# Attention scores of two window pairs computed in every second step, side by side in the same PSUM banks

## What is computed

```python
xw = windows_of_16x16(group_norm(x))                # 64 windows per image
q, k, v = [layer_norm(shuffle_invert(conv3(xw, w, b))) for w, b in ...]   # 64 tokens, 128 features
attn = einsum('bhqd,bhkd->bhqk', q * SCALE, k)      # 8 heads of 16 features: the scores
attn = softmax(attn + bias)
out = einsum('bhqk,bhkd->bhqd', attn, v) @ proj_w.T + proj_b
xr = windows_back(xw + pixel_shuffle(out))
y = xr + conv3(gelu(conv3(xr, c1w, c1b)), c2w, c2b)
x = x + y
```

## Time and profile before

| | |
|---|---|
| median of 3 runs | 852.24 us (850.86 to 852.25) |
| the profiled execution, its own time | 853.24 us |
| its span on the core | 851.1 us |
| PE busy in the span | 89% |
| DVE, ACT, POOL busy | 78%, 71%, 57% |
| mean granted TensorE clock | 0.984 |
| steps 7 to 27 of image 1 (five rows of four steps) | 287.3 to 378.0 us of the span |

### The profile page before, as it was taken

How to read it: one execution, slowest core, us unless ns; L and a number is a source line. 1 busy time by engine, 2 the same in 40 slices (tenths; PEclk the granted TensorE clock), 3 DMA queues, 4 the chain that set the end, 5 groups by cost and what they waited for, 6 DMA issues and landing times.

```text
span 851.1 us, 19126 instructions
## 1 busy us (share of the span) xinstructions
PE 761.1 (89%) x5704; PEld 537.6 (63%) x5704; DVE 660.4 (78%) x2142; ACT 605.7 (71%) x1287; POOL 483.2 (57%) x1041
## 2 busy tenths in 40 slices
PE   0479999999788999999888999999989899999988
PEld 0347777766356777767445777776735677777753
DVE  6558888878657888878675888887866788888575
ACT  1498888765478888876457888877556888886651
POOL 5468677752237777764144776776233677776410
PEclk9999999999999999999999999999999999999999
DMA  7110123000231030300052013110014212000004
GB/s 250 56 29 30 48 108 106 1 1 1 87 125 55 28 128 0 106 1 2 1 166 70 29 30 126 52 55 1 1 56 137 64 34 78 0 1 2 1 1 148
DMA packets 17655, 47.14 MB, mean 55 GB/s; under 512 B 2080, under 2 KB 2720, under 8 KB 17568
## 3 DMA queue, kind: packets, MB, share of 16 engines
q1 hardware_dynamic: 17568, 46.09, 16.6%
HBM read 37.69 MB, written 8.39 MB: 54 GB/s over the span
## 4 chain that ended last, share of the span: by engine, by line
PE 44%; issue 19%; DVE 16%; POOL 11%; ACT 8%; DVEq 1%; DMA 0%; SPq 0%; ACTq 0%; POOLq 0%
PE y_ps L998 12%; PE o_ps L1065 7%; PE pt_ps L1055 5%; PE s_ps L1044 5%; POOL ln_rs L715 4%; PE s_ps L1087 4%; DVE ln_st L540 3%; ACT qk_n L840 3%; PE ox_ps L1014 3%; PE y_ps L969 2%; ACT sc L855 2%; PE t_ps L1023 2%; ACT v_bd L848 2%; DVE h_hi L509 2%; PE y_ps L993 1%
## 5 line engine op out<-in xcount | busy, mean ns | idle before, releaser
L840 ACT ACTIVATE qk_n<-y_ps,ln_nr,ln_rs 128x128 f32<-128x128 f32 x256 | 103.5, 456 | 81.8 <-POOL ln_nr L718 81.1
L998 PE MATMUL y_ps<-w_hi,x_hi 128*128 128x192 f16 (+1 forms) x512 | 149.9, 293 | 0.0
L998 PE MATMUL y_ps<-w_hi,x_lo 128*128 128x192 f16 (+1 forms) x512 | 149.5, 292 | 0.0
L998 PE MATMUL y_ps<-w_lo,x_hi 128*128 128x192 f16 (+1 forms) x512 | 149.5, 292 | 0.0
L728 POOL TENSOR_TENSOR sc<-sc,mx 128x512 f32<-128x512 f32 x128 | 133.7, 1045 | 22.0 <-DVE mx L566 21.5
L1065 PE MATMUL o_ps<-v_bd,pt 128*128 128x66 f32 x1024 | 128.6, 268 | 0.0
L1065 PEld LDWEIGHTS o_ps<-v_bd,pt 128*128 128x128 f32 x1024 | 124.5, 192 | 0.2
L551 DVE TENSOR_TENSOR sc<-s_ps,biasS 128x512 f32<-128x512 f32 x128 | 86.5, 676 | 47.4 <-PE s_ps L1044 45.4
L540 DVE BATCH_NORM_STATS2 ln_st<-y_ps 128x6 f32<-128x128 f32 x384 | 88.7, 286 | 42.6 <-PE y_ps L998 35.5
L715 POOL TENSOR_TENSOR ln_rs<-ln_ve,neg_half 128x3 f32<-128x3 f32 x128 | 113.0, 883 | 10.7
L711 POOL TENSOR_TENSOR ln_ve<-ln_mv,eps_y 128x3 f32<-128x3 f32 x128 | 24.8, 194 | 154.1 <-DVE ln_mv L545 153.8
(11 more groups left out here) (161 smaller groups left out, 1636.5 us busy)
## 6 DMA issues: line engine op xcount, KB each, us to landing
xs<-in_x_sh_dram SPq DMA_DIRECT2D x32, 576.0 KB, 3.9
xst<-in_x_al_dram SPq DMA_DIRECT2D x16, 512.0 KB, 6.8
xf<-in_x_al_dram SPq DMA_DIRECT2D x32, 256.0 KB, 4.2
out_dram<-xf SPq DMA_DIRECT2D x32, 256.0 KB, 2.4
wst<-in_wqkv_dram SPq DMA_DIRECT2D x1, 768.0 KB, 3.8
w1s<-in_w_dram SPq DMA_DIRECT2D x1, 256.0 KB, 8.7
w2s<-in_w_dram SPq DMA_DIRECT2D x1, 256.0 KB, 8.7
biasS<-in_bias_t_dram SPq DMA_DIRECT2D x1, 256.0 KB, 9.4
```

The source lines that it names most:

```text
L840: ins = act.activation(qk_n[j][:, t, :].rearrange("p (h y x) -> p h y x", h=HEADS, y=2), by_head(y_ps[j][:, E * t:E * (t + 1)]), ACT.Identity,
L998: ins = pe.matmul(y.rearrange("p (t e) -> p t e", t=3)[:, :, cols], xx[r % 2][:, s, a % 2, 2 * TS * (a // 2):2 * TS * (a // 2 + TS)], ww[: ...
```

## The change

In an even step i, PE now computes the scores of pairs i and i+1 in one piece: pair i into columns 0 to 255 of the two banks of `s_ps`, pair i+1 into columns 256 to 511. In an odd step it computes no scores. The semaphore `scores_done` is still raised once for each pair. PE waits with the piece until the bias of pair i-1 has been added, as before. DVE reads columns 0 to 255 in even steps and 256 to 511 in odd ones. Since the two pairs lie in the same banks, DVE now waits in an even step until the scores of both pairs are there; in an odd step that wait has been met long before.

```diff
                 if has(i):
-                    v.wait_ge(scores_done, p0 + (i + 1))
+                    v.wait_ge(scores_done, p0 + (i + 2 - i % 2))
...
-                                    s_ps[:, :, 0:256], biasS[:, :, :], ALU.add).then_inc(biased, 1)
+                                    s_ps[:, :, 256 * (i % 2):256 * (i % 2) + 256], biasS[:, :, :],
+                                    ALU.add).then_inc(biased, 1)
...
-                if has(i):
+                if i % 2 == 0 and has(i):
                     h = i // 2
                     pe.wait_ge(qkt_done, h0 + (h + 1))
...
-                    if i >= 1:
+                    else:
                         pe.wait_ge(biased, p0 + i)
-                    for w in range(2):
-                        for half in range(2):
-                            rows = slice(64 * half, 64 * half + 64)
-                            out = s_ps[:, half, 0:256].rearrange("p (h k w) -> p h k w", h=2, w=2)
-                            ins = pe.matmul(out[:, :, :, w],
-                                            q_m[h % 2][rows, i % 2, w, :, :].rearrange("p a t -> p (a t)"),
-                                            k_m[h % 2][rows, i % 2, w, :, :], start=True, stop=True)
-                    ins.then_inc(scores_done, 1)
+                    for k in range(2):
+                        for w in range(2):
+                            for half in range(2):
+                                rows = slice(64 * half, 64 * half + 64)
+                                out = s_ps[:, half, 256 * k:256 * k + 256].rearrange("p (h k w) -> p h k w", h=2, w=2)
+                                ins = pe.matmul(out[:, :, :, w],
+                                                q_m[h % 2][rows, k, w, :, :].rearrange("p a t -> p (a t)"),
+                                                k_m[h % 2][rows, k, w, :, :], start=True, stop=True)
+                        ins.then_inc(scores_done, 1)
```

## The result

The changed kernel took **858.68 us** (median of 4 runs, 858.16 to 860.13) against 852.25 us (850.86 to 852.36) before: a ratio of 1.0082 with a 95% interval of 1.0064 to 1.0099. It is slower, by 6.4 us, and 0.5 us from the forecast. The profiled execution took 858.7 us with a span of 856.6 us, 5.5 us over the span before.

The account below looks back on a forecast made before the run. Two nearly level loops through PE, DVE, POOL and ACT were taken to bound the kernel. Per image 1.27 + 0.58 - 0.35 = +1.50 us, four images +6.0, from 852.24 to 858.2 us; range 851.5 to 862.5.

Parts of the forecast that it names:

- The waits say more than the busy shares: Whole kernel: PE is busy 89%, but its recurring short waits mean another chain ends level with PE's own work.
- The piece adds 0.44 us, a couple saves 0.31: PE's scores: an even step grows by 0.44 us, an odd one loses 0.75, saving 0.31 in each of 64 couples.
- The odd step's 0.75 us turns into a wait for the exponential: Steps 11, 15, 19: the removed 0.75 us becomes a PE wait for ACT's exponential; L1055 starts no earlier.
- The stretch becomes 7.73 us, statistics 0.04 us behind it: L1055 to the second convolution's end grows from 7.29 to 7.73 us; DVE's statistics follow 0.04 us later.
- Five rounds +1.27 us: Steps 7 to 27 of an image: five four-step rounds, mean 0.25 us longer each, add 1.27 us.
- Steps 28 to 31, -0.35: End of an image: the first couple saves 0.06 us, the next some 0.29, together 0.35 us less.
- Start of an image, +0.58: First steps of an image: step 2's block costs 0.44 us, step 4's 0.14 after 0.3 us of slack.
- The signs: Changed profile: odd-step L1055 waits 0.3 to 0.7 us, DVE's score wait under 15 us, round 18.3, stretch 7.73.
- PE's saving (832 us): Rival: PE's 64 x 0.31 = 20 us saving arrives in full, giving 832 us; faster had chance 0.13.
- DVE's saving being passed on: Rival: earlier bias shortens each of 20 rounds by 0.3 us, giving 852 us; no change, both kinds, 0.12.
- the rest: Part of a round from DVE's statistics over POOL and ACT to the next L1055, kept at 10.53 us.
- The end of an image: Rival: transfer waits there absorb the delay but the last image's 1.5 us, 853.7 us; no change, both kinds, 0.12.

Follow-up runs that it names:

- x_dup: Kernel before, with the score matmuls of even steps issued twice over and those of odd steps left where they are; 869.82 us, ratio 1.0186.
- x_split: Kernel before, with the odd pair's score block moved unmerged to the end of the even step, DVE's waits staying short; 867.89 us, ratio 1.0174.
- a_exp2: Changed kernel, exponential put ahead of the layer norm of v on ACT only in steps 2, 6, ..., 26; 846.04 us, ratio 0.9940 to the kernel before.
- x_noodd: Kernel before, with the scores of odd pairs left out, so it no longer computes the attention; 840.9 us, ratio 0.9872.
- a_ox: Changed kernel, in steps 4k+2 exponential ahead of v's layer norm and output transpose ahead of merged scores; 846.22 us, ratio 0.9921 to the kernel before.

## Why the prediction was right, step by step

- **The waits say more than the busy shares.** PE lost 15.4 us of work and the kernel gained 6.4 us. Right.
- **The piece adds 0.44 us, a couple saves 0.31.** 1.29 - 0.85 = 0.44 in step 12. Right.
- **The odd step's 0.75 us turns into a wait for the exponential.** 0.71 us in step 15, 0.70 in step 19, while I named 0.3 to 0.7. Right for steps 4k+3; in steps 4k+1 the waits are 0.15 to 0.40 us. There the reason was wrong: I wrote that ACT has no gap between 316.01 and the exponential, and passed over the one before `ot` (a row left out in the earlier trace rows), of 0.22 us in step 14 and 0.29 in step 18. x_dup shows what the freed time is worth there, 0.26 us a round. It stayed hidden because the later merged block of step 18 takes nearly the same back: 10.47 us for the 10.53 that I had kept. Two terms that my sum didn't have, about -0.3 and +0.25 us a round, cancelled; that part of the close forecast is luck.
- **The stretch becomes 7.73 us, statistics 0.04 us behind it.** To the digit in the round at 334.31; in the rounds over steps 13 and 21 it is 0.12 us, though DVE's own queue has ended before the convolution there too, and why stays open. A round of 18.3: 18.24 to 18.51 us.
- **Five rounds +1.27 us.** +1.24, with +1.19 to +1.24 in all four images.
- **Steps 28 to 31, -0.35.** -0.50 in each image: up to L1057 of step 29 the first couple saves 0.17 us where I had left 0.06, and steps 29 to 32 save 0.33 where I had 0.29.
- **Start of an image, +0.58.** The mean over steps 3 to 7 is +0.83, over all of the start +0.66 (3.30 - 0.66 us in four images): right in size, but by luck. By place I had 0.44 us up to step 3, where the mean of the four images is -0.17, and 0.14 from there to step 7, where it was 0.83; the slack of 0.3 us in that term stood in no row. Two drops of the clock fewer and shifted waits are in these numbers too.
- **The signs.** DVE's wait for the scores was to fall from 45.4 us to under 15, and is 36.7. That was a miss: I counted the odd steps' waits that vanish and forgot that the even steps now wait too, for both blocks (13 waits in the steady steps of image 1, 5.4 us). That this wait isn't what costs, as I had written elsewhere, x_split bears out.
- **The rivals.** PE's saving (832 us) did not arrive, and a_exp2 shows what part of it was waiting for. DVE's saving being passed on was seen as no more than the 0.06 us of the rest. The end of an image did not absorb the delay: most of the shift passes through each (the last row of the table above), and the last image alone does not make it.

## What to carry over

An engine that is busy for 89% can have most of a saving turned into a wait; take the round apart (which engine ends last at each hand-over) and ask in which part of it each piece of the edit falls. Work moved between two steps of a loop counts where it is put, not by the sum: here 1.5 us a round came out of places of which only 0.50 were worth anything (x_noodd), and of the two pieces of 0.44 us put in, one counted whole and the other with 0.25. Then an exchange of two instructions on the engine that is waited for, worth nothing in the kernel before, turned the loss of 6 us into a gain of 5 to 7: try a change that frees an engine together with the one that shortens what it will wait for.

## What the runs showed that I had not expected

- Seven tiny matmuls in the set-up made the kernel before 0.28% (0.12 to 0.43) slower, with every steady round unchanged to 0.02 us. For the changed kernel the two ratios, taken at different times, differ by 0.4%, and their intervals (1.0064 to 1.0099 and 1.0099 to 1.0139) just touch. On this kernel a difference of 2 to 3 us between two programs need not come from the work that was changed: waits of PE for nothing that the profile shows (up to 2.1 us at a time) differ between them.
- Executions of one program differ by up to 5 us with the granted clock, so a median of a few can hide 2 us that the trace shows, as with a_ox.
- A wait that the profile gives as 0.17 us, or not at all, was 0.29 and 0.24 us long: ACT's instructions overlap those ahead of them, and only the distance between the starts (1.21 and 1.16 us from the copy of k to `ot`, against 0.92 in x_noodd and 0.90 in a_ox) shows it.
